# Attention and routed feed-forward on one core: eight turns of score tiles in a row, small turns right behind them

## The reference

```python
x = x + xattn(layernorm(x), ctx, ctx, mask, wq, wk, wv, wo)
x = x + moe_ffn(layernorm(x), ...)

def xattn(query, key, value, mask, wq, wk, wv, wo):
    Q, K, V = heads(query @ wq), heads(key @ wk), heads(value @ wv)   # 16, 2, 2 heads of 32
    Q, K = rope(Q), rope(K)
    scores = einsum('bhqd,bhkd->bhqk', Q, K) / sqrt(32)
    attn = softmax(where(mask == 0, -1e9, scores), axis=-1)
    return merge(einsum('bhqk,bhkd->bhqd', attn, V)) @ wo
```

## Time and profile before

| | us |
|---|---|
| median of 3 runs | 1408.04 |
| the profiled execution | 1408.64 |
| its span, first to last instruction | 1406.8 |
| attention bodies (42.53 to 740.90) | 698.37 |
| feed-forward part (740.90 to 1406.80) | 665.90 |
| TensorE busy, whole span | 1339.5 (95%) |
| ScalarE busy | 836.6 (59%) |
| VectorE busy | 959.3 (68%) |
| chain that ended last | TensorE 73%, ScalarE 11%, VectorE 5%, issue 3%, DMA 3%, GpSimd 3%, SyncE 2% |

### The profile page before, as it was taken

How to read it: one execution, slowest core, us unless ns; L and a number is a source line. 1 busy time by engine, 2 the same in 40 slices (tenths; PEclk the granted TensorE clock), 3 DMA queues, 4 the chain that set the end, 5 groups by cost and what they waited for, 6 DMA issues and landing times.

```text
span 1406.8 us, 28203 instructions
## 1 busy us (share of the span) xinstructions
PE 1339.5 (95%) x8061; PEld 1025.5 (73%) x8061; DVE 959.3 (68%) x2665; ACT 836.6 (59%) x1951; POOL 581.3 (41%) x724
## 2 busy tenths in 40 slices
PE   6898999999999999999898999999999999999997
PEld 4675776767767677676565777777778888888885
DVE  6888989888897888988776666666653433334332
ACT  2788979889798897988983222222213333334332
POOL 3443433434344253342254333333343555555553
PEclk9799999999999999999999999999999999999999
DMA  6545464564644646545366232222257879786552
GB/s 205 149 134 152 130 193 144 144 200 136 193 144 134 201 138 181 153 139 162 104 199 216 73 101 85 82 89 84 76 174 183 216 160 279 193 196 106 111 77 37
DMA packets 145780, 206.53 MB, mean 147 GB/s; under 512 B 35295, under 2 KB 72799, under 8 KB 145634
## 3 DMA queue, kind: packets, MB, share of 16 engines
q1 hardware_dynamic: 124274, 166.84, 38.7%
q0 software_dynamic: 17952, 33.64, 12.7%
q10 hardware_dynamic: 3408, 4.26, 0.9%
HBM read 105.42 MB, written 69.35 MB: 124 GB/s over the span
## 4 chain that ended last, share of the span: by engine, by line
PE 73%; ACT 11%; DVE 5%; issue 3%; DMA 3%; POOL 3%; SPq 2%; DVEq 0%; POOLq 0%; ACTq 0%
PE psum L1505 13%; PE psum L1507 13%; PE psum L1506 13%; PE psum L695 7%; PE psum L810 6%; ACT a_probs L593 6%; PE psum L789 6%; ACT a_probsT L599 3%; PE psum L740 3%; PE psum L742 3%; PE psum L741 3%; PE psum L1572 1%; PE psum L1601 1%; PE psum L710 1%; DVE a_probs L957 1%
## 5 line engine op out<-in xcount | busy, mean ns | idle before, releaser
L593 ACT ACTIVATE a_probs<-a_probs,a_low 128x512 f32<-128x512 f32 x512 | 366.4, 716 | 82.3 <-DVE a_low L957 82.0
L957 DVE CUSTOM_DVE_ANT_0 a_probs<-psum,a_bias 128x512 f32<-128x512 f32 x512 | 343.7, 685 | 70.3 <-PE psum L789 66.9
L695 PEld LDWEIGHTS psum<-a_ident_r,a_probs_bits 128*128 128x128 f32 x2048 | 225.8, 142 | 88.1 <-issue 28.2
L695 PE MATMUL psum<-a_ident_r,a_probs_bits 128*128 128x128 f32 x2048 | 247.1, 245 | 14.9 <-ACT a_probsT L599 8.6
L789 PE MATMUL psum<-a_kT,a_q_stack 128*128 128x512 f32 x512 | 245.7, 481 | 13.4 <-DVE a_low L957 7.7
L599 ACT ACTIVATE a_probsT<-psum 128x512 f32<-128x512 f32 x328 | 189.9, 580 | 5.4 <-PE psum L695 4.7
L1374 POOL DMA_INDIRECT out<-b_y,b_pairs_sb x71 | 112.6, 1586 | 149.8 <-DMA out<-b_y,b_pairs_sb 79.8
L963 DVE COPY a_probsT<-psum 128x512 f32<-128x512 f32 x184 | 126.0, 685 | 2.8 <-PE psum L695 1.7
L1807 DVE SCALAR_TENSOR_TENSOR b_v_hidden<-b_v_hidden,psum 128x256 f32<-128x256 f32 x71 | 29.9, 421 | 134.3 <-ACT b_v_hidden L1470 89.5
L810 PE MATMUL psum<-a_probsT,a_v 128*32 128x512 f32 x1024 | 117.7, 600 | 0.0
L1505 PE MATMUL psum<-b_w,b_vT_hi 128*128 x284 | 116.6, 410 | 0.0
(11 more groups left out here) (221 smaller groups left out, 2973.1 us busy)
## 6 DMA issues: line engine op xcount, KB each, us to landing
b_w<-w_halves SPq DMA_DIRECT2D x16, 1536.0 KB
a_q_stack<-a_qT_hi SPq DMA_DIRECT2D x254, 64.0 KB, 2.0
a_q_stack<-a_qT_lo SPq DMA_DIRECT2D x253, 64.0 KB, 2.0
w_halves<-a_w_hi SPq DMA_DIRECT2D x96, 128.0 KB, 2.0
w_halves<-a_w_lo SPq DMA_DIRECT2D x96, 128.0 KB, 1.9
a_xT_in<-in_x_turned SPq DMA_DIRECT2D x32, 256.0 KB, 2.9
a_ctx_in<-in_ctx SPq DMA_DIRECT2D x32, 256.0 KB, 3.0
a_x_in<-in_x SPq DMA_DIRECT2D x32, 256.0 KB, 3.2
```

What stands on the lines that cost most here:

```text
L593: nc.scalar.activation(probs[:, h % 2, t], probs[:, h % 2, t], ACT.Exp, bias=low[:, h % H, t:t + 1], scale=-1.0, accum_out=total[:, h // G ...
L695: last = nc.tensor.transpose(out[:, P * i:P * (i + 1)].bitcast(F32R), src(i), ident_r[:])
L957: nc.vector.tensor_tensor_reduce(probs[:, h % 2, t], psum[:, t % 2], bias[:, t], 1.0, HUGE, ALU.add, ALU.min, low[:, h % H, t:t + 1]).then ...
```

## The change

Units are taken in pairs. TensorE turns unit u and unit u + 1 in a row, eight transposes; right behind them come the small turns (`kT`, `qT`, `inverse`) of both units; then the score of unit u + 6 and the other work of unit u, then the score of unit u + 7 and the other work of unit u + 1. The list `line`, and with it the order in which banks are taken, follows. The programs of the other four engines and the tables stay as they are.

```diff
+    TURNED = ("kT", "qT", "inverse")
+
+    def beside_pair(u):
+
+        first, second = PE_AT.get(u, ()), PE_AT.get(u + 1, ())
+        turns = [p for p in first + second if p[0] in TURNED]
+        return turns, [p for p in first if p[0] not in TURNED], [p for p in second if p[0] not in TURNED]
+
     line = []
-    for u in range(H * TT):
-        line.append(("probs", u))
-        line += [(kind, i) for kind, i in PE_AT.get(u, ()) if kind in RINGED]
+    for u in range(0, H * TT, 2):
+        turns, first, second = beside_pair(u)
+        line += [("probs", u), ("probs", u + 1)]
+        line += [(kind, i) for kind, i in turns + first + second if kind in RINGED]
...
-        def beside(part, b, par, u):
-            for kind, i in stages(part, PE_AT, u):
+        def beside(part, b, par, u, places):
+            for kind, i in places:
+                if not there(part, kind, i):
+                    continue
...
-            for u in range(H * TT):
-                turn_probs(part, b, u // TT, u % TT)
-                if u + AHEAD < H * TT or part != "last":
-                    scores(b, par, (u + AHEAD) // TT, u % TT ^ 2)
-                beside(part, b, par, u)
+            for u in range(0, H * TT, 2):
+                turns, first, second = beside_pair(u)
+                for w in (u, u + 1):
+                    turn_probs(part, b, w // TT, w % TT)
+                beside(part, b, par, u, turns)
+                for w, others in ((u, first), (u + 1, second)):
+                    if w + AHEAD < H * TT or part != "last":
+                        scores(b, par, (w + AHEAD) // TT, w % TT ^ 2)
+                    beside(part, b, par, w, others)
```

## The result

The changed kernel takes 1473.24 us (median of 4, 1466.48 to 1473.59) against 1407.93 before on the same chip: a ratio of 1.0456, interval 1.0433 to 1.0478. Slower, as forecast, but by 65 us where 18 stood in the sum, and outside the range that ended at 1442. The profiled execution took 1472.99 with a span of 1471.2. Two executions further down, 1615.59 and 1779.63 us at a granted clock of 0.75 and 0.65, were in a slower state of the chip and are left out of the times.

What follows compares the result with a forecast made beforehand. TensorE was taken as full (busy 85.33 of 87.59 us a body), with little lead between engines. Six middle bodies at +2.5 (15.0), first +0.9, last +1.8 gave +17.7 us, so 1426 us; range 1404 to 1442.

Steps and rivals of the forecast that it cites:

- the sign of ScalarE's wait: ScalarE's wait for VectorE's scores was to rise from 76.9 towards 95 us.
- pairs that wait for nothing: Bursts and scores on TensorE: a pair costs 1.17 us instead of 1.18, so 0.3 us a body gained.
- 1, both ends of a body: End of a body: `qT` 5 waits for copy(60), delaying the last products and the next body's start: +0.6 us.
- 2, after the weighted sum: VectorE and ScalarE are dry there; T3 now stands ahead of S72, making it later: +0.3 us.
- 3, `inverse` -1, units 8 and 9: Unit 8: `inverse` -1 waits for copy(7), holding S14 and its exponential: +0.7 us.
- 4, `qT` 2: Unit 16: `qT` 2 and two scores stand behind copy(14), where T17 and one score stood: +0.2 us.
- 5, `inverse` 0: Unit 24: `inverse` 0 waits for copy(23): +0.3 us, between 0.2 and 0.8.
- 6, `kT` 0, units 28 and 29: Unit 28: `kT` 0 waits for copy(27), with two scores and six products behind it: +1.0 us.
- 7, `kT` 1, units 34 to 37: Unit 35: TensorE's later arrival recovers its 0.8 us wait for GpSimd, less 0.53 for two scores: -0.3 us.
- The clock: Rival: new stalls at `kT` 0 and `inverse` -1 cause one more clock fall in seven bodies: 1441 us; chance 0.20.
- Theory C: Whole kernel, tested in the experiments: the number of clock falls, nine against five, goes with the time.
- The faster rival: If ScalarE catches up, banks come free in time: 1381 us at most, 1395 with half of each gain; chance 0.12.

Runs made afterwards that it cites:

- queues in pairs: Changed kernel, with ScalarE and VectorE making both copies of a pair ahead of both exponentials or lowest values: 1425.93 us, ratio 1.0116.
- half copies: Changed kernel, ScalarE copying only 256 of 512 columns of its turned units in middle and last bodies: 1451.24 us, ratio 1.0314.
- own places: Changed kernel, every small turn back beside its own unit, behind that unit's score: 1443.16 us; the same with both engines' queues paired too: 1413.13 us.

## Why the prediction was wrong

Right were the direction, the place (banks of the ring, scores behind small turns), the sign of ScalarE's wait and the prices: eight turns take 0.65 (568.79 to 569.44), a score that doesn't stand behind turns 0.23 (442.25, behind `spread`). The 15 pairs of a body that wait for nothing give 0.2 us together; the forecast had 0.3 for all 32. The Trainium skill ("TensorE: Matmul & The Clock Gate", "Back-to-back issue gap") has about 81 ns for such a matmul; 0.65 / 8 is just that, and it is the four turns alone, at 0.29, that run under it.

The steps, for the sixth body, at a clock of 1.00 in both traces (87.88 and 95.75 long; each is the change in the time between starts of two units' turns, so TensorE's own shift):

| step | forecast | measured |
|---|---|---|
| pairs that wait for nothing | -0.3 | -0.2 |
| 1, both ends of a body | +0.6 | +0.2 (+0.5 at unit 62, -0.3 at unit 0) |
| 2, after the weighted sum | +0.3 | 0.0 (+0.4, given back at unit 6) |
| 3, `inverse` -1, units 8 and 9 | +0.7 | +1.65 |
| `spread` -1, units 10 and 11 | none | +0.25 |
| 4, `qT` 2 | +0.2 | +0.35 |
| units 20 to 23 | none | +0.75 |
| 5, `inverse` 0 | +0.3 | -0.95 |
| 6, `kT` 0, units 28 and 29 | +1.0 | +1.65 |
| 7, `kT` 1, units 34 to 37 | -0.3 | +1.9 |
| `inverse` 1, `spread` 1 | 0 | +0.95 |
| `inverse` 2, `spread` 2 | 0 | +1.25 |
| sum | +2.5 | +7.9 |

**The step that failed** is the one sentence that put the other small turns at 0 "while ScalarE doesn't fall further behind", and with it the way in which every step was made: I took the copies' times from the trace of before and asked when a small turn meets them. But the copies are behind exponentials in ScalarE's queue, those behind lowest values in VectorE's, and those need the scores that the small turn holds. A wait for a copy makes the copy after the next one late. Step 3 shows it: `inverse` starts when the step said, 13.07 us into its body for 13.00, and the exponential of S14 too, 14.68 (440.34 - 425.66) as forecast (408.20 - 393.52). There the step ended. But copy(9) stands behind that exponential, and comes at 15.40 (441.06 - 425.66) where before it came at 14.64 (408.16 - 393.52), here in the timeline of ScalarE, before and after:

```profile
408.16 0.57 ACT L599 ACTIVATE a_probsT<-psum 128x512 f32<-128x512 f32 x1
```

```profile
441.06 0.58 ACT L608 ACTIVATE a_probsT<-psum 128x512 f32<-128x512 f32 x1
```

For this copy `spread` then waits, with S17 behind it. The 1.65 of units 8 and 9 is also more than the step's 0.7 because the step counted ScalarE's shift alone: on TensorE T9 waits 0.72 for copy(6) and `inverse` 0.69 for copy(7) in the sixth body. I never named `spread`; it has the largest share of the waits for copies (16.2 of 51.5 us). By the list `line` and the table `DVE_EVACUATES`, three of the four spreads of a body took the bank of a turn that VectorE copied (T8, T40, T56), and in pairs take that of the next turn, which ScalarE copies (T9, T41, T57). Of the 5.4 us a body beyond the forecast the terms put at nothing, with the spreads, hold 2.45, step 7 holds 2.2 and steps 3 and 6 hold 1.6; the rest is -0.9. The queues in pairs, with the same work and the same places on TensorE, show that the rise hangs on the order of the queues; that one wait makes the next is read from the chains at units 8 to 10 and 40 to 42.

The sentence that a small turn's bank "is that of T(u-1)" holds only where another entry of the ring stands between (`kv`, `spread` or a small turn); with none between, at units 16, 32, 56 and 63, it is T(u-2). Steps 1 and 4 have it so, and the sum is none the worse.

**Step 7** had the wrong sign. I let TensorE's lateness pay the wait for GpSimd; that wait rose instead, from 5.4 to 8.4 us, in seven bodies instead of five. In the third, fifth and sixth body the chain comes to `kT` 1 from GpSimd's part of the rotation of `q` (in the sixth 575.69 to 576.98) and from VectorE's before that (574.17 to 575.62), behind a lowest value; GpSimd's waits for that rotation are 8.9 us, where they were 0.7. So what feeds GpSimd came later too. That was not tried by itself, and the queues in pairs leave 6.3 of the 8.4 us. **Step 5** is wrong the other way: the wait of T25 for the bank of `kv` 1 (0.8 us in the sixth body) went. **Steps 1 and 2** were too dear by 0.7 together; the pair's first turns start without the score of their unit ahead, and give 0.3 back at units 0 and 6.

**The clock** was the rival I feared most and is a small part. Middle bodies at 1.00 take 95.75, those at 0.97 or 0.98 take 96.97 to 99.24: 7.5 us over four bodies, where before it was some 4 over two; the last body has 0.90 for 0.96, and what that is worth of its 5.8 us is not told apart. Theory C falls too: the granted clock of the whole execution is 0.979 in the profiled run of the change and 0.976 in that of the queues in pairs, which took 40 us less. The Trainium skill (the same page, "A second HAM failure mode: psum-queue depth-cycling") would have such waits between groups of matmuls make the clock fall: the third and sixth body, with some 8.7 us of idle time in bits of up to 1.7, stay at 1.00 and don't agree.

**The faster rival** asked for ScalarE to catch up. It had the idle time for it, but with the half copies, which gave it more, it waited longer (164.8 us for 137.3) and 41 of the 65 us stayed: in a loop idle time is no reserve.

Open: what of the 17 us left with the queues in pairs is the small turns' place and what the rest (own places bring it to 4, and the first body from 91.15 to 87.14); why units 20 to 23 take 0.75 more; and the share of VectorE's rotations of `q`, which stand in the chain ahead of `kT` 1 and were not moved.

## What to carry to other kernels

When one engine's order is bunched, the queues of those that serve it have to be bunched alike (47 of 65 us here): a copy that stands behind an exponential in its queue comes only after what that exponential waits for. Before a wait is priced by the releaser's time in the old trace, follow that releaser back on its own engine; if the path comes back to what the wait holds up, the price can be paid again in every round. Test it by reordering the queue with the work unchanged, since making the late instruction shorter (24 us of 65) or its engine less loaded shows less.

## What the runs showed of the hardware

A copy of 256 columns took 367 ns on ScalarE and one of 512 took 585, so half the columns save 37%, not half. A score right behind a small turn, unit by unit, cost nothing that the runs can tell (1411.57, ratio 1.0008, interval 0.9983 to 1.0034).
